# Another order of work on TensorE in one batch, and on five engines in the last two batches, of a graph attention kernel

## The reference

```python
h = jnp.maximum(_layernorm(x, axis=-1), 0.0)
q = _heads(h @ Wq + bq); k = _heads(h @ Wk + bk); v = _heads(h @ Wv + bv)
scores = jnp.einsum('bhqd,bhkd->bhqk', q, k) / np.sqrt(HEAD_SIZE)
probs = jax.nn.softmax(scores + where(adj, 0, -9e15)[:, None], axis=-1)
ctx = jnp.einsum('bhqk,bhkd->bhqd', probs, v)      # heads joined again
return x + (ctx @ Wf + bf)
```

## Time and profile before

| | |
|---|---|
| three executions | 589.86, 590.62, 590.72 us; median 590.62 |
| the profiled execution | 591.8 us, of which the span of the trace is 590.0 |
| PE busy | 573.5 us, 97% of the span |
| ACT busy | 516.1 us, 87% |
| POOL busy | 491.3 us, 83% |
| DVE busy | 473.8 us, 80% |
| DMA: the queue that SP issues | 79.6% of 16 engines |

### The profile page before, as it was taken

How to read it: one execution, slowest core, us unless ns; L and a number is a source line. 1 busy time by engine, 2 the same in 40 slices (tenths; PEclk the granted TensorE clock), 3 DMA queues, 4 the chain that set the end, 5 groups by cost and what they waited for, 6 DMA issues and landing times.

```text
span 590.0 us, 17760 instructions
## 1 busy us (share of the span) xinstructions
PE 573.5 (97%) x6640; PEld 428.9 (73%) x6640; DVE 473.8 (80%) x1484; ACT 516.1 (87%) x1161; POOL 491.3 (83%) x533
## 2 busy tenths in 40 slices
PE   7997999999999999999999999999999999999977
PEld 7676777777777777777777777777777777777755
DVE  4988788888888888878888887887877778787775
ACT  1788999899999999999999999999999999999882
POOL 2779998888998888899888889988888988888960
PEclk9999999999999999999999999999999999999999
DMA  8047889788888978899988877899988788987584
GB/s 273 10 77 140 133 169 184 158 169 167 156 156 165 176 162 168 174 129 174 179 167 170 162 169 150 158 183 156 183 162 159 151 159 181 160 157 143 72 162 117
DMA packets 275641, 92.01 MB, mean 156 GB/s; under 512 B 257634, under 2 KB 275555, under 8 KB 275555
## 3 DMA queue, kind: packets, MB, share of 16 engines
q1 hardware_dynamic: 274352, 90.87, 79.6%
q10 hardware_dynamic: 1202, 0.01, 0.1%
HBM read 17.05 MB, written 12.58 MB: 50 GB/s over the span
## 4 chain that ended last, share of the span: by engine, by line
PE 80%; DVE 6%; ACT 5%; DMA 5%; issue 2%; POOL 2%; ACTq 0%; SPq 0%; DVEq 0%; POOLq 0%
PE ring L1106 18%; PE ring L1108 18%; PE ring L1107 18%; PE scores L1169 11%; PE ctx L1195 5%; PE ring L1207 3%; PE ctx L1197 3%; PE ctx L1196 3%; DMA p_cols<-p_rows 3%; ACT probs L574 2%; DVE logits L796 1%; DVE h_rows L813 1%; DMA bf_row<-in_L_gnn_bf_dram 1%; ACT qk L602 1%; POOL p_rows L440 1%
## 5 line engine op out<-in xcount | busy, mean ns | idle before, releaser
L440 POOL TENSOR_TENSOR p_rows<-probs,p_rows 128x512 f16<-128x512 f32 x190 | 220.6, 1161 | 30.2 <-ACT p_rows L582 29.8
L796 DVE CUSTOM_DVE_ANT_0 logits<-scores,mask,logit_unscale 128x256 f32<-128x256 f32 x384 | 169.1, 478 | 57.5 <-PE scores L1169 57.3
L574 ACT ACTIVATE probs<-logits,raised 128x256 f32<-128x256 f32 x372 | 168.9, 501 | 6.1
L1106 PE MATMUL ring<-h_cols,w_hi 128*128 128x256 f16 x576 | 157.2, 273 | 0.0
L1108 PE MATMUL ring<-h_cols,w_lo 128*128 128x256 f16 x576 | 157.0, 273 | 0.0
L1107 PE MATMUL ring<-h_cols,w_hi 128*128 128x256 f16 x576 | 156.9, 272 | 0.0
L426 POOL TENSOR_TENSOR split<-qk,split 128x512 f16<-128x512 f32 x96 | 111.4, 1160 | 36.4 <-DVE split L820 36.4
L582 ACT ACTIVATE p_rows<-probs 128x512 f16<-128x512 f32 x190 | 119.6, 630 | 5.9
L602 ACT ACTIVATE qk<-ring,qk_bias_s,qkv_ratio 128x256 f32<-128x256 f32 x192 | 96.5, 552 | 3.9 <-PE ring L1108 3.8
L1195 PEld LDWEIGHTS ctx<-v_hi,p_cols 128*128 128x128 f16 x756 | 69.0, 97 | 33.9 <-issue 26.1
L1195 PE MATMUL ctx<-v_hi,p_cols 128*128 128x65 f16 x756 | 88.1, 195 | 5.5 <-DMA p_cols<-p_rows 4.1
(11 more groups left out here) (116 smaller groups left out, 1155.7 us busy)
## 6 DMA issues: line engine op xcount, KB each, us to landing
x_in<-in_x_dram SPq DMA_DIRECT2D x32, 384.0 KB, 3.8
out_dram<-result SPq DMA_DIRECT2D x62, 192.0 KB, 2.2
p_cols<-p_rows SPq DMA_TRANSPOSE x190, 3.2
adj_in<-in_adj_dram SPq DMA_DIRECT2D x32, 64.0 KB, 2.6
w_raw<-in_L_gnn_Wq_dram SPq DMA_DIRECT2D x1, 576.0 KB, 6.1
w_raw<-in_L_gnn_Wv_dram SPq DMA_DIRECT2D x1, 576.0 KB, 7.9
w_raw<-in_L_gnn_Wf_dram SPq DMA_DIRECT2D x1, 576.0 KB, 9.0
h_cols<-h_rows SPq DMA_TRANSPOSE x29, 4.8
```

Source lines behind the costliest of these rows:

```text
L440: pool.tensor_tensor(p_rows[u][:, 1], probs[u % 3][:], p_rows[u][:, 0], ALU.subtract).then_inc(p_lo_ready, 1)
L574: act.activation(probs[u % 3][:, a], logits[u % 3][:, a], ACT.Exp, bias=raised[u % 3][:, a:a + 1], scale=-1.0).then_inc(probs_ready, 1)
L796: dve.tensor_tensor_reduce(out=logits[u % 3][:, a], in0=score_bank[a][:, u % 2 * S:(u % 2 + 1) * S], in1=mask[b.parity][:, t], scale=logit ...
L1106: pe.matmul(out_ap, a_hi, m_hi, start=first, stop=False)
```

## The change

On PE batch 1 no longer goes through `cycle`, which now begins with batch 2; its steps stand written out in another order. The steps and their matmuls are the same. On all five streams some steps of the part behind `cycle(29)` change places: on SP `store(PREV + -2, 0)` comes first, and the other stores come behind more transposes. The core of the diff:

```diff
-            for k in range(1, B - 2):
+            for k in range(first, B - 2):
...
@@ SP
+            store(PREV + -2, 0)
             transpose_probs(PREV + -1, 4)
             transpose_probs(PREV + -1, 5)
             transpose_probs(PREV, 1)
             transpose_probs(PREV, 0)
-            store(PREV + -2, 0)
             transpose_probs(PREV, 2)
+            transpose_probs(PREV, 3)
             store(PREV + -2, 1)
+            transpose_probs(PREV, 4)
             store(PREV + -1, 0)
-            transpose_probs(PREV, 4)
-            transpose_probs(PREV, 3)
-            store(PREV + -1, 1)
             transpose_probs(PREV, 5)
             transpose_probs(LAST, 0)
             transpose_probs(LAST, 1)
             transpose_probs(LAST, 2)
             transpose_probs(LAST, 3)
+            store(PREV + -1, 1)
...
@@ POOL
-            add_bias(LAST)
             probs_lo(PREV + -1, 5)
             make_mask(LAST)
-            split_lo(LAST, 0)
+            add_bias(LAST)
             probs_lo(PREV, 0)
             probs_lo(PREV, 1)
             probs_lo(PREV, 2)
+            split_lo(LAST, 0)
+            split_lo(LAST, 1)
             probs_lo(PREV, 3)
-            split_lo(LAST, 1)
             raise_last(0)
...
@@ ACT
             qk_full(LAST, 0)
+            probs_hi(PREV, 0)
             exps(PREV, 1)
-            probs_hi(PREV, 0)
...
+            qk_full(LAST, 1)
             exps(PREV, 3)
             probs_hi(PREV, 3)
-            qk_full(LAST, 1)
+            exps(PREV, 4)
+            context_hi(PREV + -1, 1)
+            probs_hi(PREV, 4)
             qk_full(LAST, 2)
...
@@ DVE
             mask_and_max(PREV, 0)
+            mask_and_max(PREV, 1)
+            v_lo_part(PREV, 0)
             divide(PREV + -1, 0)
...
             mask_and_max(PREV, 5)
+            mask_and_max(LAST, 0)
             finish(PREV + -1, 0)
             context_lo(PREV + -1, 1)
-            mask_and_max(LAST, 0)
-            v_lo_part(LAST, 0)
...
@@ PE
+            scores(Batch(1), 0)
+            apply_probs(Batch(0), 2)
+            project_qk(Batch(2), 0)
+            apply_probs(Batch(0), 3)
+            scores(Batch(1), 1)
+            project_qk(Batch(2), 1)
+            apply_probs(Batch(0), 4)
+            transpose_context(Batch(0), 0)
+            scores(Batch(1), 2)
+            apply_probs(Batch(0), 5)
+            project_qk(Batch(2), 2)
+            apply_probs(Batch(1), 0)
+            pe.wait_ge(w_lo_ready, 8)
+            project_out(Batch(0), 0)
+            project_v(Batch(2), 0, (0,))
+            apply_probs(Batch(1), 1)
+            transpose_context(Batch(0), 1)
+            project_v(Batch(2), 0, (1, 2))
+            project_v(Batch(2), 1)
...
-            cycles(cycle)
+            cycles(cycle, 2)
...
+            apply_probs(PREV + -1, 3)
             scores(PREV, 1)
-            apply_probs(PREV + -1, 3)
...
+            project_out(PREV + -1, 0)
             transpose_context(PREV + -1, 1)
-            project_out(PREV + -1, 0)
+            apply_probs(PREV, 0)
             project_v(LAST, 0, (0,))
-            apply_probs(PREV, 0)
...
+            apply_probs(PREV, 2)
             project_v(LAST, 1)
-            apply_probs(PREV, 2)
...
             transpose_context(LAST, 0)
+            apply_probs(LAST, 5)
             transpose_context_last(UP_TO, 2)
-            apply_probs(LAST, 5)
```

More of the change, by code:

```diff
@@ L267, in gnn_attention, with cycles @@
         BY_PE = 3
-        def cycles(cycle):
-            for k in range(1, B - 2):
+        def cycles(cycle, first=1):
+            for k in range(first, B - 2):
                 cycle(Batch(k))
@@ L745, in _ @@
             probs_hi(PREV, 2)
+            qk_full(LAST, 1)
             exps(PREV, 3)
             probs_hi(PREV, 3)
-            qk_full(LAST, 1)
+            exps(PREV, 4)
+            context_hi(PREV + -1, 1)
+            probs_hi(PREV, 4)
             qk_full(LAST, 2)
-            exps(PREV, 4)
-            probs_hi(PREV, 4)
-            context_hi(PREV + -1, 1)
             exps(PREV, 5)
             v_hi_part(LAST, 0)
+            probs_hi(PREV, 5)
             exps_last(0)
-            probs_hi(PREV, 5)
+            probs_hi(LAST, 0)
             v_hi_part(LAST, 1)
-            probs_hi(LAST, 0)
             exps_last(1)
@@ L1058, in _ @@
             mask_and_max(PREV, 0)
+            mask_and_max(PREV, 1)
+            v_lo_part(PREV, 0)
             divide(PREV + -1, 0)
-            mask_and_max(PREV, 1)
+            finish(PREV + -2, 1)
+            v_lo_part(PREV, 1)
             qk_hi_part(LAST, 0)
-            finish(PREV + -2, 1)
-            v_lo_part(PREV, 0)
             mask_and_max(PREV, 2)
-            v_lo_part(PREV, 1)
             mask_and_max(PREV, 3)
-            context_lo(PREV + -1, 0)
             divide(PREV + -1, 1)
             mask_and_max(PREV, 4)
+            context_lo(PREV + -1, 0)
             qk_hi_part(LAST, 1)
             mask_and_max(PREV, 5)
+            mask_and_max(LAST, 0)
             finish(PREV + -1, 0)
             context_lo(PREV + -1, 1)
-            mask_and_max(LAST, 0)
-            v_lo_part(LAST, 0)
             qk_hi_part(LAST, 2)
@@ L1081, in _ @@
             mask_and_max(LAST, 3)
+            v_lo_part(LAST, 0)
             context_lo(PREV, 0)
@@ L1088, in _ @@
             turned_lo(4, 1)
+            finish(PREV, 0)
             divide(LAST, 0)
-            finish(PREV, 0)
             turned_lo(5, 2)
@@ L1308, in cycle @@
                 attend(4)
-                if b.k == 1:
-                    pe.wait_ge(w_lo_ready, 8)
                 if before:
```

## The result

The changed kernel takes 594.17 us (median of four, 593.99 to 594.31) against 590.55 of the kernel before on the same chip: +3.6 us, ratio 1.0058 with an interval of 1.0042 to 1.0073. Measured again on another chip it is 1.0045 (1.0023 to 1.0067), +2.7 us. The forecast was 593.0 us, slower by 2.4. A ratio and its interval (95%) are formed over all executions of both kernels, so it need not equal the quotient of the two medians; three executions of over 900 us, none of them of the changed kernel itself, are left out.

What follows compares the result with a forecast made beforehand. TensorE was taken to bound the kernel, busy 97% of the span. Work left behind the stall +2.33, clock +1.2 and end -1.1 sum to +2.4 us, moving the median from 590.62 to 593.0 us; range 590.4 to 595.1.

Steps and rivals of the forecast that it cites:

- What bounds it, and where there is room: Whole kernel: TensorE full from 81 to 520 us; room only in batch 1's cycle (3.7 us) and last batches (3.6 us).
- The stall before scores(1, 2): Cycle of batch 1: scores(1, 2) waits for mask_and_max(1, 3), PE idling from about 52.7 to 57.6, some 4.9 us.
- 2.33 us of work left behind it: Cycle of batch 1: apply(0, 5) and qk(2, 2), queued behind the waiting scores, remain to be done, costing +2.33 us.
- The clock, +1.2: Around the stall in batch 1's cycle: one fall of TensorE to 1.2 GHz, costing +1.2 us, bounds 0 and 1.7 or 2.
- that case with 2 us: Clock bound for the stall in batch 1's cycle: idle time before 51.8 adds a second half-clock stretch, costing 2 us.
- The end, -1.1: Last two batches: the 2.01 us wait before apply(PREV, 5) goes almost wholly, net -1.1 us, bounds 0 and -3.6.
- the one that I had put at +0.1: Last batches up to scores(LAST, 2): some 0.6 us wait before apply(PREV, 0) replaces small gaps, net +0.1 us.
- The passage on what is late next: Last batch: transposes of LAST are late next; PE reaches apply(LAST, 3) at 580.2, 1.1 us earlier.
- (a): Stall comes but clock holds, or the end gains 2 us instead of 1.1: +1.2, 591.9 us; chance 0.17.
- (b): All 3.6 us of waits at the end go, stall and clock as forecast: -0.1, 590.6 us; chance 0.11.
- (c): Faster: shorter h_lo_rows(3) pair shortens batch 1's stall, cycle loses 0.5, end gains 2.0: -1.5, 589.1 us; chance 0.10.
- (d): The end loses its 1.1 us gain and the clock takes 1.7 to 2: +4.2, 594.8 us; chance 0.12.

Runs made afterwards that it cites:

- e5: Changed kernel with mask_and_max(1, 3) on DVE moved ahead of context_lo(0, 0) and h_lo_rows(3): 590.95 us against 590.87 for the kernel before, ratio 1.0008.
- e3: Changed kernel with 13 products of zeros on TensorE between transpose_context(0, 0) and scores(1, 2): 590.33 us, ratio 0.9979 to the kernel before.
- after: The changed kernel as first measured and profiled, both parts of the change: 594.17 us, ratio 1.0058 to the kernel before.
- e1: Kernel before with only TensorE's new order in the cycle of batch 1: 594.15 us against 591.18, ratio 1.0040.
- after_again: The changed kernel unaltered, measured again on another chip: 593.02 us against 590.87 for the kernel before, ratio 1.0045.
- e2: Kernel before with only the new orders of the last two batches: 590.64 us against 591.18, ratio 0.9984.
- e4: Changed kernel with scores(1, 2) moved back behind apply(0, 5) and qk(2, 2): 591.55 us against 591.18 for the kernel before, ratio 0.9997.
- e9: Kernel before with new end, project_v(LAST, 0) first, and SP's load for batch 4 behind the transposes of (0, 4) and (0, 5): 591.74 us, ratio 0.9997.
- before: The kernel before the change, as first profiled and compared with the changed kernel: 590.55 us.
- before_again: The kernel before, unaltered, measured and traced a second time: 591.57 us against 591.22, ratio 1.0002.
- e10: Changed kernel with 6 products of zeros on TensorE between transpose_context(0, 0) and scores(1, 2): 591.36 us, ratio 1.0003 to the kernel before.
- e12: Kernel before with new end, project_v(LAST, 0) ahead of apply(PREV, 0), but SP's end in its old order: 592.36 us against 591.22, ratio 1.0011.
- e8: As e5, with SP's load of x for batch 5 behind the transposes of (1, 1) and of h for batch 3: 590.53 us, ratio 0.9997.

## Why the prediction was right, point by point

- **What bounds it, and where there is room.** Right. 81 to 520 us were full in both kernels, and in the profiled pair the delay of the first cycle, 22.3 - 19.8 = 2.5 us, arrived whole at the end: scores(PREV, 0) starts at 551.63 against 549.22.
- **The stall before scores(1, 2).** Right in each link. Forecast was an idle time of 4.9 us, from 52.7 to 57.6; measured are 3.95, because the pair of h_lo_rows took 2.05 us instead of 2.99. e5 shows that the place of mask_and_max(1, 3) on DVE is the cause.
- **2.33 us of work left behind it.** Right: at full clock scores(1, 2) to scores(2, 0) takes 8.66 us in e3 and 6.35 in the old order, a difference of 2.31.
- **The clock, +1.2.** Right in kind, too small: 1.32, 1.95 and 2.45 us in three traces (after, e1, after_again), mean 1.9. In the last two half clock was granted for 6.8 us in all instead of 3.4. I had named that case with 2 us and taken it for the less likely one. The record of the other executions agrees: none of the 22 of the changed kernel and of e1 has a mean granted clock above 0.997, while of the 98 of the kernel before beside the experiments 44 have 1.000.
- **The profiled execution as a base.** A term that the forecast lacked. Its pair of h_lo_rows was the slowest of all traces; with the usual 2 us the old cycle takes 18.9 to 19.0 us instead of 19.8. I used 2.99 us for both kernels and carried the difference of the traces over to the medians. By the usual rows the cycle loses 22.9 - 19.0 = 3.9 us (mean of after, after_again and e1): 2.3 + 1.9, less 0.3 since scores(1, 2) starts 12.3 and not 12.6 us after scores(1, 0). That the two profiled spans differ by 2.3 us, close to the forecast 2.4, is luck: scores(1, 2) came 1.15 us sooner after scores(1, 0) than in the trace before (12.30 against 13.45), which the forecast did not have, and the end gave 0.1 us instead of 1.1.
- **The end, -1.1.** The direction was right, as e2 shows (0.1 to 1.8 us faster), the size too large by the traces: over the eight of them with the new end and apply(PREV, 0) first it takes 36.1 to 37.7 us, median 37.4, against 37.8 in the three with the old one: -0.4. The second half, from scores(LAST, 0), gains 0.9 us as against 1.2 forecast. The step that failed is the one that I had put at +0.1: up to scores(LAST, 0) it takes 0.5 us longer (median 15.25 against 14.74). PE waits for the transpose of (PREV, 0) with nothing to do, where project_v had filled that time. I had seen this wait, put it at 0.6 us, and netted it against small gaps that did not go. The passage on what is late next was right: the waits before apply(LAST, 0) and (LAST, 2), 0.46 and 0.52 us, ate half of what apply(PREV, 5) gave.
- **Sum.** 3.9 - 0.4 = +3.5; measured +3.6 on the first chip and +2.7 (1.4 to 4.0) on the second; forecast +2.4. The time came out right in direction and inside the range, but 1.2 us low on the first chip, by two terms that were both too favourable, the clock by 0.7 us and the end by 0.7, less the 0.3 just named.
- **The rivals.** (a) and (b) needed a clock that holds or an end that gives 2 or 3.6 us: neither came. (With an end of -2 the sum of (a) is +1.5, not the +1.2 written there.) (c), a short pair of h_lo_rows, did occur (1.3 us in e4 and e9), though in no trace of the changed kernel; there it took 2.05 and 1.97. My ground for dropping it, that the 1.5 us of each instruction would stay because POOL's steps do not move, failed: POOL was busy without a gap and only one of the two took 1.5 us. Nor would a short pair have made the change faster by what the runs show: with the stall gone altogether, in e5, the time is 1.0008 times that of the kernel before, as PE then waits for the transpose of (1, 1), which I had not priced at all. (d), the end giving nothing and the clock 1.7 to 2, at 594.8 us, lies nearer to the measured 594.17 than the forecast does, and it had the end of the profiled pair right, where the two differ by 0.1 us.

## What to carry to other kernels

Before a step is moved ahead of others, look up what it waits for on the engine that releases it: what matters is not only how long that work takes but where it stands in that engine's order, and whether one of the steps before it waits for the very step after which the waiter was put. An idle time that is filled earlier is worth something only up to the next arrival that the same path needs; here a transpose that landed at 59.8 to 60.6 us took back all that three different orders had gained. Waits are not priced by their length alone: one that left the clock at full cost its length, the one of 3.95 us here cost its length and, on the mean of three traces, 1.9 us of slowed work on top. And a forecast formed as a difference against one trace carries that trace's oddities with it: a second trace of the kernel before would have shown that the pair of 2.99 us was one.

## What the runs showed of the hardware that was not expected

- Idle times of TensorE of nearly the same length did and did not lower its clock. Single waits of 2.01, 1.96 and 2.53 us (before, before_again, e10) left it at 1.00; one of 2.06 (e12) and one of 2.39 (e4) were followed by half clock; the stall of 3.9 to 4.0 us was in all three traces that have it, with 2.8 us (after), 4.2 (e1) and 5.1 (after_again) of the work behind it at half clock. A kernel with waits near 2 us can so pay in some executions and not in others. The record of single executions fits this: of the ten of before_again the four with a mean granted clock of 1.000 took 590.3 to 590.9 us, the three with 0.997 took 591.2 to 592.4, the three with 0.994 took 591.9 to 592.5. The spread goes with the clock; where in the kernel the low stretches lie is known for the profiled executions only. The Trainium skill ("TensorE: Matmul & The Clock Gate", Part 1) has an idle array fall to 1.2 GHz; at 4 us the traces agree each time, at 2 us only some of them do.
- Two equal DVE instructions at the same place, h_lo_rows(3), took 1.3 to 3.0 us as a pair in otherwise like kernels, with POOL busy beside them. Each of the two took either 0.54 to 0.72 us or 1.50 to 1.56: one was long in ten of the fourteen traces, none in e4, e8 and e9, both in the first trace of the kernel before. The runs do not show why.
- Single transposes by DMA took 4.8 to 5.6 us at the start of the pipeline ((0, 4) before; (1, 1) in e4, e5 and e9) in place of the median 3.2. In e8, with a load of 384 KB moved behind it, that of (1, 1) took 4.7 at the most against 5.5 in e5, one trace each.
